# The last layer's attention in units of two head groups on TensorE tiles

## The reference

```python
def _L3_attn_ref(x, qkv_weights):
    H = 16; Dh = D // H                      # D = 128, Dh = 8
    qkv = jnp.einsum('bsd,de->bse', x, qkv_weights)
    q, k, v = ...
    k = jnp.transpose(pre_k, (0, 2, 3, 1)).reshape(-1, S, Dh)
    a = jnp.einsum('aib,ajb->aij', q, k) / sqrt(Dh)
    a = tril * a + NEG_INF * (1.0 - tril)
    a = jax.nn.softmax(a, axis=-1)
    heads = jnp.einsum('aij,ajb->aib', a, v)
```

## Time and profile before

| | |
|---|---|
| Median of 3 runs | 5986.1 us |
| Lowest and highest run | 5985.38 and 5986.49 us |
| Span of the profiled execution | 5995.4 us |
| TensorE busy | 4804.1 us, 80% |
| VectorE busy | 3795.6 us, 63% |
| ScalarE busy | 3211.5 us, 54% |
| GpSimd busy | 1986.0 us, 33% |
| Mean granted clock of TensorE | 0.902 |

### The profile page before, as it was taken

The page is one execution under the profiler, slowest core; times in us unless marked ns, Lnnn a source line. Parts: engine busy times, 40 slices in busy tenths (PEclk is TensorE's granted clock), DMA queues, the critical chain, the costliest instruction groups (busy, mean ns, idle before and its releaser), DMA issues. The chain is left out here.

```text
span 5995.4 us, 91995 instructions
## 1 busy us (share of the span) xinstructions
PE 4804.1 (80%) x27408; PEld 3412.1 (57%) x27408; DVE 3795.6 (63%) x8398; ACT 3211.5 (54%) x9294; POOL 1986.0 (33%) x1579
## 2 busy tenths in 40 slices
PE   6888897999864446888888888888888887688888
PEld 4667664666631104566666666666666665466666
DVE  5555223444558886777777777777777776455522
ACT  4444343555323335666666766666766665244433
POOL 3333100222204553444444444444444442122200
PEclk8888998999975558999999999999999999688899
DMA  0000000000000001000000000000000000000000
GB/s 16 1 2 2 33 0 19 2 2 2 13 3 0 0 0 47 1 0 21 0 0 21 0 0 21 0 0 21 0 0 0 0 0 1 16 1 0 0 28 7
DMA packets 26030, 41.55 MB, mean 7 GB/s; under 512 B 12208, under 2 KB 18376, under 8 KB 25160
## 3 DMA queue, kind: packets, MB, share of 16 engines
q1 hardware_dynamic: 25800, 38.86, 1.9%
HBM read 36.75 MB, written 2.10 MB: 6 GB/s over the span
## 5 line engine op out<-in xcount | busy, mean ns | idle before, releaser
L1380 PE MATMUL ps<-l2f_wqkv,l2f_xsT 128*128 (+3 forms) x1536 | 741.6, 606 | 96.5 <-DVE xnT L1575 90.5
L1312 POOL TENSOR_TENSOR l2f_rn<-l2f_ss,neghalf 128x16 f32<-128x16 f32 x192 | 564.7, 2941 | 436.2 <-DVE l2f_ss L1569 436.2
L1757 ACT ACTIVATE l2f_p<-ps,l2f_negmax 128x96 f32<-128x96 f32 x1536 | 501.7, 339 | 281.8 <-DVE l2f_negmax L1600 278.2
L1318 POOL TENSOR_TENSOR l2f_cosd<-xnT,l2f_rot 128x1024 f32<-128x1024 f32 x192 | 487.0, 2541 | 174.8 <-DVE xnT L1575 174.8
L1438 PE MATMUL ps<-l2f_pT,l2f_vw 96*128 96x128 f32 x3072 | 419.7, 280 | 39.2 <-DVE l2f_pT L1622 38.9
L1380 PEld LDWEIGHTS ps<-l2f_wqkv,l2f_xsT 128*128 128x128 f32 (+1 forms) x1536 | 243.4, 178 | 347.4 <-issue 197.2
L1772 ACT COPY l2f_oT<-ps 64x256 f32<-64x256 f32 x768 | 281.3, 366 | 268.1 <-PE ps L1438 256.4
L1438 PEld LDWEIGHTS ps<-l2f_pT,l2f_vw 96*128 96x128 f32 x3072 | 379.4, 194 | 59.4 <-issue 54.2
L1338 POOL TENSOR_TENSOR l2f_rstd<-l2f_mv,neghalf 128x1 f32<-128x1 f32 x96 | 52.8, 550 | 1045.9 <-DVE l2f_mv L1634 1045.9
L1411 PEld LDWEIGHTS ps<-l2f_kT,l2f_qz 128*128 128x128 f32 x3072 | 398.3, 194 | 1.5 <-issue 0.4
L1411 PE MATMUL ps<-l2f_kT,l2f_qz 128*128 128x96 f32 x3072 | 397.9, 273 | 0.0
(11 more groups left out here) (348 smaller groups left out, 12274.8 us busy)
## 6 DMA issues: line engine op xcount, KB each, us to landing
l2f_wqkv<-L_ffn_Wqkv_dram SPq DMA_DIRECT2D x18, 512.0 KB
l0f_w<-L_w_dram SPq DMA_DIRECT2D x2, 2304.0 KB
l3f_w<-L_w_dram SPq DMA_DIRECT2D x2, 2048.0 KB
l2f_wo<-L_ffn_Wo_dram SPq DMA_DIRECT2D x6, 512.0 KB
l2f_w<-L_ffn_W_dram SPq DMA_DIRECT2D x6, 341.0 KB
l2f_b<-L_ffn_b_dram SPq DMA_DIRECT2D x6, 341.0 KB
l1f_w<-L_w_dram SPq DMA_DIRECT2D x1, 1152.0 KB
k_turn<-l3a_kF SPq DMA_DIRECT2D x4, 256.0 KB, 2.0
```

Source lines behind the costliest of these rows:

```text
L1312: nc.gpsimd.tensor_tensor(rn[:, k], ss[:, k], g.neghalf[:, 0:HEADS], ALU.pow).then_inc(rn_ready, 1)
L1318: nc.gpsimd.tensor_tensor(cosd[:, k].rearrange("p (h d) -> p h d", d=DH), nrm[:, k].rearrange("p (h d) -> p h d", d=DH), rot[:, k, 0, t].u ...
L1380: ins = nc.tensor.matmul(g.ps[0:rows, 2 * (k % 2) + hf], x, wqkv[:, bass.ds(weight_slot(it), 1), c0 + hf * 512:c0 + (hf + 1) * 512] .rearr ...
L1757: ins = nc.scalar.activation(p[:, n % 2, c], g.ps[:, 4, c * KW:(c + 1) * KW], ACT.Exp, bias=negmax[:, col:col + 1], accum_out=rowsum[:, co ...
```

## The change

A new class PairSoftmax takes the place of Softmax in this stage. The 16 heads are taken as four lanes of 32 features, four heads each. A unit is two such groups (h = 0, 1) of 4 heads by 32 queries; two units make a block of 32 queries, so a batch has 16 blocks, 32 units. All of a block's units have 32 * (block + 1) keys.

- The scores of a group use 32 feature rows of q and k (lane(n, h)), on one of two 32-row tiles of TensorE. Group 0 writes one PSUM bank, group 1 the next. From 384 keys on they come in two pieces, split at 256 keys, the groups taking turns. The mask comes from two small tables in the same lane.
- The values of a group use 32 of the 128 value columns, so that the output lies on 32 rows of one bank, PV_BANK, on one of two 32-column tiles. Four groups fill the bank, and one product with a table of four heads serves two units.
- The maximum, the inverse and the scaling are one instruction for both groups; the exponential is one for each group.
- Group 0's turned probabilities are copied by VectorE, group 1's by ScalarE.
- TensorE's list becomes scores(n + 2), values(n - 1), turns(n). VectorE's becomes inverse(n), maximum(n + 2), copy(n - 1), collect(n - 2). Scores have two buffers instead of three.
- Turned pieces always have 128 rows. p is cleared by GpSimd in each batch instead of once by VectorE.

```diff
+    def pe_scores(self, pe, b, n):
+        pe.wait_ge(self.probs_ready, self.at(b, 0 if n < 2 else n if self.big(n) else n - 1))
...
+        for i, (c0, c1) in enumerate(pieces):
+            for h in range(2):
+                ins = nc.tensor.matmul(s[:, h, c0:c1], self.q(n, h), self.k(n, h, c0, c1),
+                                       start=self.mask_before is None or i > 0, stop=c1 <= m0 or self.mask_before is not None)
...
+    def pe_pv(self, pe, b, n):
+        pe.wait_ge(self.copied[0], self.at(b, n + 1))
+        pe.wait_ge(self.copied[1], self.at(b, n + 1))
+        pe.wait_ge(self.collected, self.at(b, n // self.every * self.every))
+        chunks = self.chunks(n)
+        for c in range(chunks):
+            for h in range(2):
+                ins = self.nc.tensor.matmul(self.g.ps[self.lane(n, h), self.PV_BANK, 0:P], self.v(n, h, c),
+                                            self.pT[:, n % 2, h, c * P:(c + 1) * P],
+                                            start=(c == 0), stop=(c == chunks - 1))
+    def tensor(self, pe, b):
+        self.pe_scores(pe, b, 0)
+        self.pe_scores(pe, b, 1)
+        for n in range(self.units):
+            self.pe_scores(pe, b, n + 2)
+            self.pe_pv(pe, b, n - 1)
+            self.pe_turn(pe, b, n)
+        self.pe_pv(pe, b, self.units - 1)
+    def vector(self, dve, b):
+        self.maximum(dve, b, 0)
+        self.maximum(dve, b, 1)
+        for n in range(self.units + 2):
+            if n < self.units:
+                self.inverse_sum(dve, b, n)
+            self.maximum(dve, b, n + 2)
+            if 1 <= n <= self.units:
+                for h in range(2):
+                    if self.copiers[h] == "dve":
+                        self.copy_turned(dve, self.nc.vector.tensor_copy, b, n - 1, h)
+            if n >= 2 and self.collector == "dve":
+                self.collect(dve, b, n - 2)
+PIECE = 256
...
-        qz = sb("qz", [P, SEQ // QB, HEADS, QB])
+        qz = sb("qz", [P, BLOCKS, PER, QB])
-        own = sb("own", [P, 2, GROUP, HEADS, QB])
+        own = sb("own", [P, 2, GROUP, PER, QB])
+        def lane(n, h):
+            return slice((2 * (n % 2) + h) * QB, (2 * (n % 2) + h + 1) * QB)
+
+        at = PairSoftmax(g, sb, sem, units=2 * BLOCKS, keys=lambda n: QB * (n // 2 + 1), lane=lane,
+                         q=lambda n, h: qz[lane(n, h), n // 2].rearrange("p h q -> p (h q)"),
+                         k=lambda n, h, c0, c1: kT[lane(n, h), c0:c1], v=lambda n, h, c: v[:, c, lane(n, h)],
+                         mask_before=None, mask_after=lambda n: (spread, later, QB),
+                         collect=collect, collector="dve", every=2, copiers=("dve", "act"))
-            sp.dma_start(heads[:], g.c["heads"]).then_inc(loaded, 16)
+            sp.dma_start(consts[:], g.c["fours"]).then_inc(loaded, 16)
+                nc.gpsimd.memset(at.p[:], 0.0).then_inc(p_zeroed, 1)
-            nc.vector.memset(at.p[:], 0.0).then_inc(zeroed, 1)
```

More of the change, by code:

```diff
@@ L1826, in l3_attn_stage @@
     W = D // HEADS
-    QB = P // HEADS
-    GROUP = 8
+    LANES = 4
+    PER = HEADS // LANES
+    QB = P // PER
+    BLOCKS = SEQ // QB
+    GROUP = 4
     M = SEQ // W
@@ L1832, in l3_attn_stage @@
         wq = sb("wq", [P, D])
-        heads = sb("heads", [P, HEADS])
+        consts = sb("consts", [P, PER + P + QB])
+        heads = consts[:, 0:PER]
+        spread = sb("spread", [P, P], BF16)
+        later = sb("later", [P, QB], BF16)
         wk = sb("wk", [P, D])
@@ L1856, in l3_attn_stage @@
         qz_ready = sem("qz_ready")
+        p_zeroed = sem("p_zeroed")
+        owned = sem("owned")
         summed = sem("summed")
@@ L1875, in l3_attn_stage @@
-        at = Softmax(g, sb, sem, steps=SEQ // QB, keys=lambda n: QB * (n + 1),
-                     q=lambda n: qz[:, n].rearrange("p h q -> p (h q)"), k=lambda n, c0, c1: kT[:, c0:c1],
-                     v=lambda n, c, rows: v[0:rows, c], mask=lambda n: g.causal8[:], collect=collect, copier="act")
+            if i % GROUP == 0:
+                dve.wait_ge(summed, CREDIT + b * GROUPS + i // GROUP - 1)
+            nc.vector.tensor_tensor(own[:, i // GROUP % 2, i % GROUP],
+                                    g.ps[:, at.PV_BANK, 0:P].rearrange("p (h q) -> p h q", q=QB),
+                                    heads.unsqueeze(2).broadcast_to([P, PER, QB]), ALU.mult).then_inc(at.collected, 2)
@@ new lines, in collect @@
+            if i % GROUP == GROUP - 1:
+                dve.wait_ge(at.collected, at.at(b, n + 1))
+                if i == GROUP - 1:
+                    dve.wait_ge(o_turned, CREDIT + b)
+                nc.vector.tensor_reduce(oT[:, (i - GROUP + 1) * QB:(i + 1) * QB].rearrange("p (j q) -> p j q", q=QB),
+                                        own[:, i // GROUP % 2].rearrange("p j h q -> p j q h"), AX_X,
+                                        ALU.add).then_inc(summed, 1)
+        def lane(n, h):
+            return slice((2 * (n % 2) + h) * QB, (2 * (n % 2) + h + 1) * QB)
@@ L1900, in _ @@
                 pool.wait_ge(v_ready, CREDIT + b)
+                pool.wait_ge(at.turned, at.at2(b, 0))
                 nc.gpsimd.tensor_copy(xb[:], g.xnT[:, bass.ds(b * SEQ, SEQ)]).then_inc(xb_ready, 1)
+                nc.gpsimd.memset(at.p[:], 0.0).then_inc(p_zeroed, 1)
                 at.pool(pool, b)
@@ L1935, in _ @@
             dve.wait_ge(loaded, 16 * 4)
-            nc.vector.memset(at.p[:], 0.0).then_inc(zeroed, 1)
+            nc.vector.tensor_copy(spread[:], consts[:, PER:PER + P])
+            nc.vector.tensor_copy(later[:], consts[:, PER + P:]).then_inc(zeroed, 1)
             with dve.Fori(0, BATCH) as b:
@@ L2368, in causal @@
         return np.where(np.arange(n)[None] > i[:, None] % n, np.float32(-1e30), np.float32(0))
-    heads = (i[:, None] // (D // HEADS) == np.arange(HEADS)[None]).astype(np.float32)
-    return {"ident": np.eye(P, dtype=np.float32), "causal64": causal(64), "causal8": causal(8), "heads": heads,
+    fours = np.concatenate([(i[:, None] // 8 % 4 == np.arange(4)[None]), (i[:, None] % 32 == i[None] % 32),
+                            np.where(np.arange(32)[None] > i[:, None] % 32, np.float32(-1e30), np.float32(0))], 1)
+    return {"ident": np.eye(P, dtype=np.float32), "causal64": causal(64), "causal8": causal(8), "fours": fours.astype(np.float32),
             **more_constants()}
```

151 lines of the change are left out of this document (140 added, 11 removed).

## The result

The changed kernel takes 6080.9 us (median of 4 runs, 6077.94 to 6087.2) against 5986.3 for the kernel before (5985.38 to 5995.23). The ratio is 1.015, with a 95% interval of 1.0134 to 1.0166: slower by 1.5%. The forecast was 6098, the range 5930 to 6285.

The account below looks back on a forecast made before the run. TensorE bounded the steps before; the closed chain was to make it stand each round: 153.9 against 120.5 us per batch, less 5.0 at the ends, over four batches, less 1: +112 on 5986.1 = 6098 us, range 5930 to 6285.

Parts of the forecast that it names:

- closed chain: Scores, maximum, copy, values, turns, next scores run in series; TensorE idle before L445 1.2 us at 256 keys, 2 at 512.
- The output bank: Start of a unit's values on TensorE: predicted to wait for VectorE's copy; no wait for the product was priced.
- Overlap of the tiles: Two groups' scores and values on TensorE overlap by half a step; none gives 6208 us, full 6059.
- The term for the scores: Scores of a 512-key unit on two row tiles, middle two of four instructions together: 1.09 us at clock 1.00.
- Price of a change of shape: Three tile-shape changes per unit on TensorE, about 0.20 us each at clock 1.00 and 0.30 at 0.50.
- The clock: TensorE's granted clock: 0.50 up to 256 keys and 1.00 beyond, giving 72.4 + 81.5 = 153.9 us per batch.
- rival 1: Clock low throughout because TensorE stands in every round: 199.9 us per batch, 6282 us; chance 0.20.
- The end of a batch: Last maximum to last sum, with fewer, longer stages: 8.2 us instead of 5.9, +2.3 per batch.
- The start: Queries before a batch's first score: 8.89 us to about 2.6, -6.3 per batch; memset hidden, first batch another -1.0.
- the sign: Whole kernel predicted slower, +112 us; chances slower 0.71, faster 0.21, same 0.08.

Follow-up runs that it names:

- the first experiment: VectorE's copy of the turned unit n-1 moved ahead of the maximum of unit n+2, against the changed kernel: 5918.9 us, 0.9873 of the kernel before.
- the undone overlap: Scores of both groups put on one 32-row tile, against the changed kernel: 6181.4 us (one run).
- fillers on the whole array: Two or three useless 128-row identity matmuls between scores and values in units 16 to 29, against the changed kernel: 6011.0 us, 1.0018 of the kernel before.
- fillers on 32 rows: Useless identity matmuls on 32 rows between scores and values in units 16 to 29, against the changed kernel: 6085.6 us, 1.0146 of the kernel before.

## Why the prediction was right, and where its terms were not

**The closed chain: right.** I expected TensorE idle ahead of L445 by 1.2 us at 256 keys and 2 at 512; the rows have 1.12 in a round of 256 keys and 2.15 in one of 480 (1.93 and 2.21 in the last two). Taking the maximum out of the chain's way turned +1.5% into -1.3%, and with the product also ahead into -2.6%. So without the chain there is no loss. The low clock that came with it had its part in the loss too, as the end of this section shows.

**The output bank: missed.** I had the values wait for the copy alone. They wait for the product L2086 too, which stands behind the copy. In the changed kernel this is small: the product is 0.28 us long, and rounds are 4.63 and 4.41 us in turn at 256 keys, so some 3.5 us per batch (an estimate, 16 times the difference). The group puts 88.2 us of idle time down to L2086 because it comes last, not because it costs that much. Once the copy was early it was the bound, as the first experiment showed.

**Overlap of the tiles: half a step taken, full measured.** The term for the scores, 3 x 256 + 2 x 256, should have been 4 x 256. The Trainium skill, "TensorE: Matmul & The Clock Gate", Part 3, which has matmuls on distinct row groups run concurrently, is the rule that I weighed and set aside; the undone overlap (+92 us of busy time) and the 0.91 us of scores for 480 keys bear it out.

**Price of a change of shape: over-priced.** I took 0.20 at clock 1.00 and 0.30 at 0.50 from the earlier trace rows; by the subtractions above the rounds leave 0.08 to 0.11 and 0.12 to 0.16. The drain on a change of mode that the Trainium skill has in "TensorEngine Tiling (Array Packing)", Key Properties, would be a cause of such a price; no run here takes the changes away, so the cause is not shown. In a round of 256 keys at 0.50 I had 5.62 us, and 4.41 is measured. Of the 1.21 too much, the three changes are 0.47 (0.90 less 0.43), and the overlap 0.65 (0.44 of the scores, 0.21 of the values).

**The clock: wrong in the other direction.** I kept 1.00 beyond 256 keys. It is 0.50 to 352 keys and 0.63 from there to the last maximum, so the rounds of 512 keys, which I had at 5.8 us, take 6.98. So the condition of rival 1 held nearly throughout, and its price of 6282 was wrong, since it stood on the over-priced rounds at 0.50. By halves of the third batch: up to the last maximum of 256 keys I had 72.4 us, and it took 44.5 (5487.72 to 5532.23). Beyond it I had 81.5, and it took 95.2. Of the 28 us in the first half, the cheaper rounds are about 16 (an estimate, some 1.0 us by 16 units). The rest I put down to bookkeeping: I counted each unit's values and turns in the half of its scores, but they run two to three units later.

**The end of a batch: under-priced.** From last maximum to last sum I had 8.2 us, and 13.9 is measured. Units 30 and 31 do not share their stages: each scaling of 1024 elements takes 1.89 us, after it come turns, copy and values with TensorE idle between them, and the last such run starts only when the one before is through. I had added up one unit's. On the other side I had counted the values and turns of the last two units in the 153.9 as well, so that first maximum to last sum was 162.1 in the forecast (153.9 + 8.2) and is 153.5.

**The start: right but for one wait.** Queries -6.4 (-6.3 forecast), last sum -0.9, memset hidden: as foreseen. From the arrival of the keys to the first maximum of the first batch it took 13.1 us before and takes 8.2 now. I expected 7.3 less, not 4.9: the products of queries and values, which before ran beside the transfer, now wait for the small casts that stand behind it on VectorE. The group, whose 26.9 us are that one wait:

```profile
L2143 PE MATMUL ps<-l3a_xb,l3a_wq 128*128 128x512 f32 x8 | 8.3, 1139 | 31.0 <-DVE l3a_later L2167 26.9 <-DVE s L2183 4.1
```

The four batches cost 19.7 to 22.8 us each instead of 28.4. So the forecast was near the measured time partly by luck: the rounds were priced too high by tile prices, and too low by the clock.

**Standing and clock apart.** The first to the last maximum of the third batch, in three stretches of keys, in us with the granted clock behind. The last column is the fourth batch of the kernel with fillers on the whole array.

| keys | before | changed | copy first | copy and product first | fillers, fourth batch |
|---|---|---|---|---|---|
| to 256 | 51.9 (0.61) | 44.5 (0.50) | 37.1 (0.50) | 32.4 (0.50) | 44.5 (0.50) |
| to 352 | 24.0 (1.00) | 31.6 (0.50) | 26.2 (0.51) | 20.1 (0.58) | 27.1 (0.66) |
| to 512 | 44.7 (1.00) | 63.5 (0.63) | 35.0 (1.00) | 29.4 (1.00) | 46.5 (1.00) |

```profile
5487.72:5532.23 44.51, 32.04 (x184) 18.13 (x184) 12.56 (x47) 16.08 (x73) 8.57 (x14) 0.50 0.00 0
...
5361.02:5393.45 32.43, 31.32 (x186) 18.03 (x188) 14.19 (x50) 15.74 (x73) 8.57 (x14) 0.50 0.00 0
...
5413.54:5442.92 29.38, 28.00 (x306) 21.84 (x306) 19.47 (x36) 17.46 (x51) 15.74 (x10) 1.00 0.00 0
```

These are the changed kernel to 256 keys, and the kernel with copy and product first to 256 and to 512. Up to 256 keys the clock is 0.50 in both, and TensorE is busy 32.0 and 31.3 us, so the 12.1 us between them are the standing, but for 0.7. Beyond 352 keys 17.1 us lie between two kernels at 1.00, one of which stands (46.5 and 29.4), and another 17.0 between 1.00 and 0.63 with the chain closed in both (63.5 and 46.5; the fillers may hold up the values a little, so the clock is worth at least that). The clock is thus about half of the difference in the large units. The kernel with the copy first shows its worth without any filler: its first batch took 48.9 us there at 0.65, its third 35.0 at 1.00.

It also bears on the sign. With the chain closed and the large units at 1.00 the fourth batch took 144.8 us, no longer than the 145.5 before. The forecast had the large units at 1.00 and a loss all the same, because its rounds were too dear: it named the place of the wait rightly, but for the kernel to come out slower it took the low clock besides, which the forecast did not have. That part of the sign was luck.

What stays open is why the standing lowers the clock. Each experiment that removed the standing also raised the clock, but the fillers on 32 rows took up idle time too (135.2 us ahead of the values instead of 169.7) and did not.

## What to carry to other kernels

When two engines' queues are written out by hand, draw one unit's operations as a loop through both queues: if the operation that releases the bound engine stands behind one that needs that engine's newest result, the loop is closed, and both engines take turns. Moving the releasing operation ahead left nothing out and here turned a loss of 1.5% into a gain of 2.6%. After a change that packs small tiles, compare an untouched group (here the turns, busy 162.7 us against 135.0 before) to see what the clock did, before judging the packing by the total.

## What the runs showed of the hardware that I had not expected

The granted clock did not follow TensorE's share of busy time. With the same number of extra matmuls of the same columns, 128 rows gave 0.86 in the large units of the third batch at 81% busy, and 32 rows gave 0.56 at 83%; the times were 6011 and 6086 us. Values on one column tile instead of two gave 0.81 at 72%, and the same total as the overlap, where the changed kernel has 0.63 at 71%. With copy and product first TensorE is busy 97% of the stretch to 256 keys, and the clock is 0.50. The Trainium skill, "TensorE: Matmul & The Clock Gate", Part 1, has the clock follow how busy TensorE has been; these windows show that busy time as the profile counts it does not order them. Useless work in a wait made a kernel faster by 70 us, which is less than removing the wait gave.
